# Expert tiles of the first four batches run before the last batches are ranked

## The chip, the cores and the metric

The kernel runs on one core of a Trainium2 chip. Its time is the device time in microseconds, the median of three runs: 293.11 us (292.9 to 294.67). Inputs are those of the reference.

## The reference

A gated block in two steps, on 8 batches of 256 tokens of width 512, all in float32:

```
x = x + tanh(g_xattn) * attention(layernorm(x), ctx, mask)
x = x + tanh(g_ffn)   * experts(layernorm(x))
attention: scores = h @ ctx.T / sqrt(512), -1e30 where masked, softmax, @ ctx
experts:   probs = softmax(y @ w_router.T); the two largest of 8, renormalised
           out = sum over the two of weight * (silu(y @ w_gate[e].T) * (y @ w_up[e].T)) @ w_down[e].T
```

w_gate and w_up are 192 x 512 for each expert, w_down is 512 x 192. Each of the 2048 tokens goes to two experts, so there are 4096 assignments.

## The kernel before

**Two stages.** The first stage runs over 16 tiles of 128 tokens (two a batch), in software-pipelined steps: in step s, tile s is transposed (`t1`), tile s-1 is scored, its row maximum and exponential are taken (`rowmax`, `exp`), tile s-2 has its probabilities transposed and multiplied with the context (`tp`, `pv`), tile s-3 gets the attention result added (`x2`, L655), its second norm (`stats`, `rstd`, `nbias`, `x2ln`) and its transposes (`t2`), and tile s-4 its router logits (`rt`). ScalarE's queue stores each tile of the residual to `out` and each normed tile to a DRAM table `x2s` (L450, L454).

**Ranking.** For each batch b, VectorE finds the two best experts of each token (`top2`, `ranks`), TensorE counts how many earlier assignments an expert has (`cum`), VectorE turns this into a slot number and two one-hot matrices TA and TB (`slots`, L714 and L721), and TensorE sums their products in the PSUM bank PTB (`tab`): a table that gives the token of every slot. `coefs` makes the token's weight for each expert, which SyncE stores in the last 8 columns of `x2s`. On VectorE this work is woven between the operations of the main chain (`weave`, list `side`).

**Second stage.** The slots of an expert are cut in tiles of 128. `tiles` computes from the final counts which expert and which slots each of up to 39 tiles has; this gives the index lists IXG (gather) and IXI (scatter), the experts ER, the live number LN and a bit for each tile whose expert is another than that of the tile before (TN). A tile j is then: a gather of 128 rows of `x2s` into one of 6 buffers XG (GpSimd's queue, L409), four transposes (`tx`, L1063), a split into a high and a low float32r part (`xhi`, `xlo`), twelve products with the gate and up weights (`gu`, L1073, L1074, L1077), SiLU and product (`silu`, `mul`), two transposes (`th`), another split (`hhi`, `hlo`), five products (`down`), scaling on ScalarE (`yev`, into one of 5 buffers YT) and an indirect DMA that adds the tile to `out` (GpSimd's queue, L435). TensorE's order in an iteration is gu(j), tx(j+1), down(j-1), th(j). Since two tiles of different experts can hold the same token, GpSimd waits, where the expert changes, until every earlier add has landed (`fence`, `landed`). After add j GpSimd issues gather j+6.

**Weights.** 40 pieces of 128 x 512 are loaded by SyncE (`loadw`), rounded on ScalarE (`hi`) and the rest of the rounding computed on GpSimd (`lo`, L379). SPLIT says how many fall in each step: two, and four of them only in the second stage (HOLD).

All engines run their programs in order; what sets the order is the code as written, with semaphores.

Of the kernel before, what the change touches and what calls it, by code (L numbers as in the profile page):

```python
# [8 lines left out]
NTK = 16  # L9
# [5 lines left out]
NB = 5  # L15
# [14 lines left out]
def flamingo(nc, x, ctxn, ctxt, mask, gates, wr, wgu, wd1, wd2, cst, cstb, out):  # L30
# [11 lines left out]
    with ctx:  # L42
# [32 lines left out]
        bit = CS[:, 486:525]  # L75
# [39 lines left out]
        Y2 = sb("Y2", [128, 2, D], where=a)  # L115
        Y2T = sb("Y2T", [128, KC, 128], where=a)
        WS = sb("WS", [128, 2, 512], where=a)
        TA = sb("TA", [128, 4, 128], f32r, where=a)
        TB = sb("TB", [128, 4, 128], f32r, where=a)
        mrow = sb("mrow", [B, S], mybir.dt.uint8, where=a)  # L120
        mbf = P[0:B, 0, :]
        mb = sb("mb", [128, S], bf16, where=a)
        gr = sb("gr", [B, 2], where=a)
        gt = sb("gt", [B, 2], where=a)
        va = sb("va", [B, 1], where=a)
        gv = sb("gv", [B, 10], where=a)
        mx = sb("mx", [128, 2, 8], where=a)
        ix = sb("ix", [128, 2, 8], u32, where=a)
        dd = sb("dd", [128, 2, 1], where=a)
        e2 = sb("e2", [128, 2, 1], where=a)  # L130
        den = sb("den", [128, 2, 1], where=a)
        cc = sb("cc", [128, 2, 2], where=a)
        OH = sb("OH", [128, 2, 2, E], where=a)
        pc = sb("pc", [128, 2, 2, E], where=a)
        pr = sb("pr", [128, 2, 2, E], where=a)
        sl = sb("sl", [128, 2, 2], where=a)
        Qi = sb("Qi", [128, 2, 2], i32, where=a)
        rr = sb("rr", [128, 2, 2], where=a)
# [1048 lines left out]
```

## Time and profile before

| what | value |
|---|---|
| median of 3 runs | 293.11 us |
| the profiled execution | 292.34 us |
| its span on the core | 290.5 us |
| TensorE busy | 254.5 us (88%) |
| VectorE busy | 172.3 us (59%) |
| ScalarE busy | 147.4 us (51%) |
| GpSimd busy | 163.8 us (56%) |
| mean granted TensorE clock | 0.944 |

The profile is one execution, timed from the span's start. The first stage takes about 104 us, the second runs from 135 us. Busy shares are means over both; what bounds each stretch is read from the stretch alone.

### The profile page before, as it was taken

The numbers are of one execution on the slowest core, as the hardware profiler recorded it, in microseconds if no ns is written. First come the engines' busy times: TensorE is split into PE (matmuls) and PEld (weight loads), VectorE is DVE, ScalarE is ACT, GpSimd is POOL, SyncE is SP. The second block draws the span as 40 slices with busy tenths as digits, with TensorE's granted clock in tenths as the row PEclk, the third lists the DMA queues.
The fourth block names the chain that finished last, engine by engine and source line by source line (L and its number), as shares of the span: only waits on it lengthen the run. The fifth ranks groups of instructions, "written<-read, shape, count | busy, mean of one in ns | idle before, by whom it ended". The sixth has DMA issues, their size and how long they took to land.

```text
span 290.5 us, 5453 instructions
## 1 busy us (share of the span) xinstructions
PE 254.5 (88%) x1501; PEld 216.1 (74%) x1501; DVE 172.3 (59%) x650; ACT 147.4 (51%) x310; POOL 163.8 (56%) x151
## 2 busy tenths in 40 slices
PE   0999998999999975366999999999999999999940
PEld 1777875687777645356899999899999999999920
DVE  4477779999987899970444444444444554444420
ACT  3469865787765645300455554454444455444430
POOL 1256557556564448316066686874857747748460
PEclk9999999999999978557999999999999999999985
DMA  6996999789988229006157576885985858958582
GB/s 219 381 386 192 325 353 282 295 265 336 301 302 296 82 104 287 4 1 184 38 81 145 103 136 123 143 143 94 171 178 93 168 114 143 154 98 163 109 142 36
DMA packets 25950, 52.08 MB, mean 179 GB/s; under 512 B 5248, under 2 KB 5376, under 8 KB 25920
## 3 DMA queue, kind: packets, MB, share of 16 engines
q0 software_dynamic: 8304, 19.83, 37.0%
q1 hardware_dynamic: 13008, 23.50, 24.7%
q10 hardware_dynamic: 4608, 8.39, 7.6%
q8 instruction: 15, 0.25, 0.3%
q14 instruction: 15, 0.12, 0.2%
HBM read 33.81 MB, written 17.89 MB: 178 GB/s over the span
## 4 chain that ended last, share of the span: by engine, by line
PE 63%; DVE 23%; issue 5%; ACT 3%; DMA 2%; POOL 1%; ACTq 0%; POOLq 0%; DVEq 0%
PE S L1073 9%; PE S L1074 9%; PE S L1077 9%; PE A L1063 5%; PE PO L946 4%; DVE st L609 4%; PE S L935 4%; DVE X L655 3%; DVE TB L721 3%; DVE TA L714 2%; PE PL L1096 2%; DVE dd L675 2%; PE PO L1098 1%; PE PO L1096 1%; PE PL L1100 1%
## 5 line engine op out<-in xcount | busy, mean ns | idle before, releaser
L435 POOL DMA_INDIRECT out<-YT,IXI x36 | 56.8, 1577 | 42.1 <-issue 20.1
L1073 PE MATMUL S<-WGh,XTh 128*128 x144 | 52.3, 363 | 0.9 <-issue 0.8
L1074 PE MATMUL S<-WGl,XTh 128*128 x144 | 49.3, 342 | 0.0
L409 POOL DMA_INDIRECT XG<-x2s,IXG x39 | 38.5, 986 | 18.0 <-issue 9.4
L875 DVE TENSOR_TENSOR H<-SG,S 128x192 f32<-128x192 f32 x36 | 12.7, 354 | 48.5 <-ACT SG L548 40.9
L379 POOL TENSOR_TENSOR WGl<-WGl,WGh 128x512 fp32r<-128x512 f32 x24 | 30.6, 1280 | 14.9 <-ACT WGh L504 14.8
L548 ACT ACTIVATE SG<-S 128x192 f32<-128x192 f32 x36 | 11.9, 330 | 50.3 <-PE S L1077 47.6
L370 POOL TENSOR_TENSOR rs<-mv,CS 128x1 f32<-128x1 f32 x32 | 17.6, 551 | 31.2 <-DVE mv L615 31.2
L946 PE MATMUL PO<-CX,PT 128*128 128x512 f32 x64 | 32.8, 637 | 2.0 <-ACT PT L477 2.0
L868 DVE TENSOR_TENSOR XTl<-A,XTh 128x512 fp32r<-128x512 f32 x37 | 25.6, 691 | 13.0 <-ACT XTh L541 7.9
L1077 PE MATMUL S<-WGh,XTl 128*128 x144 | 31.3, 340 | 0.0
L935 PE MATMUL S<-CT,XLT 128*128 128x256 f32 x128 | 31.0, 386 | 0.0
L1073 PEld LDWEIGHTS S<-WGh,XTh 128*128 128x128 f32 x144 | 27.5, 191 | 1.5 <-issue 1.4
L1074 PEld LDWEIGHTS S<-WGl,XTh 128*128 128x128 f32 x144 | 27.7, 192 | 0.0
L541 ACT ACTIVATE XTh<-A 128x512 fp32r<-128x512 f32 x37 | 22.1, 598 | 8.7 <-PE A L1063 4.3
L1077 PEld LDWEIGHTS S<-WGh,XTl 128*128 128x128 f32 x144 | 26.1, 192 | 0.0
L935 PEld LDWEIGHTS S<-CT,XLT 128*128 128x128 f32 x128 | 23.6, 195 | 2.9
L499 ACT ACTIVATE Y<-X,nb,rs 128x512 f32<-128x512 f32 x16 | 13.0, 812 | 22.7 <-DVE nb L624 22.6
L609 DVE BATCH_NORM_STATS2 st<-X 128x6 f32<-128x512 f32 x32 | 22.0, 688 | 3.9 <-DMA X<-in_x 3.4
L1063 PE MATMUL A<-CS,XG 128*128 128x128 f32 x148 | 22.2, 272 | 1.4 <-DMA XG<-x2s,IXG 1.4
L1063 PEld LDWEIGHTS A<-CS,XG 128*128 128x128 f32 x148 | 18.4, 140 | 2.8 <-issue 1.6
L946 PEld LDWEIGHTS PO<-CX,PT 128*128 128x128 f32 x64 | 11.6, 199 | 10.7 <-issue 8.2
(153 smaller groups left out, 535.8 us busy)
## 6 DMA issues: line engine op xcount, KB each, us to landing
WGl<-in_wgu SPq DMA_DIRECT2D x24, 256.0 KB, 6.2
X<-in_x SPq DMA_DIRECT2D x16, 256.0 KB, 5.3
CT<-in_ctxt SPq DMA_DIRECT2D x8, 512.0 KB, 6.7
CX<-in_ctxn SPq DMA_DIRECT2D x8, 512.0 KB, 5.4
out<-X ACTq DMA_DIRECT2D x16, 256.0 KB, 5.7
x2s<-Y ACTq DMA_DIRECT2D x16, 256.0 KB, 5.2
WD1l<-in_wd SPq DMA_DIRECT2D x8, 256.0 KB, 5.6
WS<-in_wd SPq DMA_DIRECT2D x8, 256.0 KB, 4.6
```

What stands on the lines that cost most here:

```text
L379: pool.tensor_tensor(out=low, in0=raw[p], in1=hi[p].bitcast(fp32), op=ALU.subtract).then_inc(s_wl, 1)
L409: pool.indirect_dma_start(out=XG[:, j % NX, :], out_offset=None, in_=x2s, in_offset=bass.IndirectOffsetOnAxis(ap=IXG[:, j:j + 1], axis=0))\
L435: pool.indirect_dma_start(out=out, out_offset=bass.IndirectOffsetOnAxis(ap=IXI[:, j:j + 1], axis=0), in_=YT[:, j % NB, :], in_offset=None, ...
L541: act.activation(XTh[:, j % 2, :, :], (A0, A1)[j % 2][:, :].rearrange("p (k c) -> p k c", k=KC), ACT.Copy).then_inc(s_xh, 1)
L609: n = mark(dve.bn_stats(st[:, k % 2, :], src))
L868: dve.tensor_tensor(XTl[:, j % 2, :, :], (A0, A1)[j % 2][:, :].rearrange("p (k c) -> p k c", k=KC), XTh[:, j % 2, :, :].bitcast(fp32), ALU ...
L935: m = pe.matmul(SC[k % 2][:, 0:S], XLT[:, k % 2, c, :], CT[:, b % 2, c, :], start=False, stop=(c == KC - 1))
L946: m = pe.matmul(PO[:, :], PT[:, k % 2, c, :], CX[:, b % 2, c, :], start=(c == 0), stop=(c == 1))
L1063: m = pe.transpose((A0, A1)[j % 2][:, 128 * c:128 * c + 128], XG[:, j % NX, 128 * c:128 * c + 128], ident)
L1073: pe.matmul(o, XTh[:, j % 2, c, :], WGh[:, bass.ds(e, 1), c, :], start=(c == 0), stop=False)
L1074: pe.matmul(o, XTh[:, j % 2, c, :], WGl[:, bass.ds(e, 1), c, :], start=False, stop=False)
L1077: m = pe.matmul(o, XTl[:, j % 2, c, :], WGh[:, bass.ds(e, 1), c, :], start=False, stop=(c == KC - 1))
```

## The change

**What it does.** The first four batches (EB = 4) have 2048 assignments over 8 experts. Whatever the routing, at least 16 - 7 = 9 tiles of these are whole (NE = 9). The change makes a first list from the counts and the table after four batches: IXE (rows), ERE (experts), the first nine entries of EJ (weights' columns) and TNE (bits). These nine tiles run first in the second stage; the ranking of batches 4 to 7, the tail of the first stage (`pv(15)`, `rt(13)` to `rt(15)`, `t2(14)`, `t2(15)`) and the second list (`left`, `last_tiles`: up to 30 tiles) run inside tiles 0 to 8. On TensorE they stand at fixed places of the loop over tiles; on VectorE SIDES gives how many operations of the list `side` follow `mul`, `coef` and `hlo` of each tile.

**GpSimd.** Gather 0 stands in step 16, gathers 1 to 5 between the last norms, gather j+8 after add j. Gather 9 is the first that needs the second list (IXG). Before add j GpSimd waits that add j-2 has landed; that add j-1 has landed only where the bit is set: where the expert changes and the last token of tile j is not before the first token of tile j-1. At add 9 it always waits for add 8.

**Weights.** Three pieces a step for 12 steps; none is left for the second stage.

**Small operations.** The factor 1/sqrt(512) is put on ScalarE's eviction of the transposed tile, the maximum is negated by the reduction itself, and the gate of the attention is put on ScalarE's eviction of the probabilities: two VectorE operations of 128 x 1 a tile fewer. For batches 6 and 7 the exponential is made on GpSimd as a power (`odds`).

**Buffers.** Tiles of the second stage use one PSUM bank for `tx` (A0), the bank of `gu` again for `th`, one for `down` (PO); YT has 7 buffers. XG lies on X, so gathers wait for the stores of X's tiles (`stored`). The filling matmuls (`warm`) of the handover are gone.

```diff
-NB = 5
+NB = 7
-SPLIT = [0, 1, 1] + [2] * 15 + [1] * 4
-NUA = NU - 4
-HOLD = [3, 5, 7, 9]
+SPLIT = [0, 1, 2] + [3] * 12 + [1]
+EB = 4
+NE = 4 * EB - 7
+SIDES = [(2, 2, 5), (2, 2, 3), (1, 1, 2), (1, 1, 2), (2, 2, 2), (2, 2, 3), (1, 3, 4), (2, 1, 4)] + [(0, 0, 0)] * 31
...
@@ GpSimd @@
+            for s in range(NTK + 1):
+                for u in units(s - 1)[0:1]:
+                    lo(u)
+                if s == NTK:
+                    pool.wait_ge(s_ixe, 1)
...
+                    stored(9, 10)
+                    gather(0)
...
             for j in range(NT):
                 with lives(pool, live, j):
+                    if j == 1:
+                        odds(7)
                     pool.wait_ge(s_y, j + 1)
-                    if j:
+                    if j >= 2:
+                        landed(j - 2)
+                    if j == NE:
+                        landed(j - 1)
+                    elif j:
                         fence(j)
...
+                    if j == 0:
+                        gather(NX)
+                        gather(NX + 1)
+                    if j + NX + 2 == NE:
+                        pool.wait_ge(s_ixg, 1)
...
+                    if j + NX + 2 < NT:
+                        gather(j + NX + 2)
...
@@ VectorE @@
             def rowmax(k):
                 dve.wait_ge(s_sc, k + 1)
-                n = mark(dve.reduce_max(nmx[:, k:k + 1], SC[k % 2][:, 0:S], AX.X))
-                yield
-                need(n)
-                dve.tensor_scalar(nmx[:, k:k + 1], nmx[:, k:k + 1], -SCALE, None, ALU.mult).then_inc(s_mx, 1)
+                dve.reduce_max(nmx[:, k:k + 1], SC[k % 2][:, 0:S], AX.X, negate=True).then_inc(s_mx, 1)
+                yield
...
+            side += [coefs(5), top2(6), taken()]
+            weave(queue(x2(14), first_xlo(), nbias(mv2, rs2, nb2, 14, s_rs2, s_nb2), x2(15)), 2)
+            side += [slots(5), ranks(6), coefs(6),
+                     braid(slots(6), queue(top2(7), braid(ranks(7), coefs(7)))),
+                     braid(slots(7), left()), last_tiles()]
...
                     mul(j)
+                    steps(SIDES[j][0])
                     if j + 1 < NT:
                         xlo(j + 1)
...
                     coef(j)
+                    steps(SIDES[j][1])
                     hlo(j)
+                    steps(SIDES[j][2])
...
@@ TensorE @@
+            tp(14)
+            first_list()
+            score(15)
+            pv(14)
+            rt(12)
+            t2(13)
+            tp(15)
...
             tx(0)
-            own, live = experts(0), None
+            pv(15)
+            rt(13)
+            own, live = experts(0, ERE, 0), None
+            pe.wait_ge(s_wl, NU)
             for j in range(NT):
                 with lives(pe, live, j):
...
                     gu(j, own[j])
+                    if j == 0:
+                        t2(14)
+                    if j == 1:
+                        t2(15)
+                        rt(14)
                     if j + 1 < NT:
                         tx(j + 1)
+                    if j == 0:
+                        cum(5)
+                    if j == 2:
+                        tab(5)
+                        cum(6)
+                    if j == 4:
+                        cum(7)
+                        count()
+                    if j == 5:
+                        tab(6)
+                    if j == 6:
+                        last_list()
+                        tab(7)
...
                     if j >= 1:
                         down(j - 1, own[j - 1])
+                    if j == 1:
+                        rt(15)
+                    if j == 6:
+                        last_rows()
                     th(j)
+                    if j == 0:
+                        tab(4)
```

**TensorE at the start of the second stage, before.** PTB is the table, sel and selE the one-hot choice of slots for each tile, XG the gathered rows.

```order
L1034 MATMUL PL<-Rn,CB 128x8
L989 MATMUL PTB<-TB,TA 128x128 [waits s_oh] x4
L1039 MATMUL PO<-sel,CS 1x40 [waits s_x2,s_sel]
L1043 MATMUL PC<-sel,Tsb 128x40 [waits s_sel]
L1044 MATMUL PL<-selE,CB 128x320
L910 MATMUL S<-CB 128x128 x32
L1063 MATMUL A<-CS,XG 128x128 [waits s_ixi,s_g0,s_wl,s_er]
L1053 TENSOR_LOAD ER
L1073 ISA [waits s_xh]
L1073 MATMUL S<-WGh,XTh 128x384
```

And in the changed kernel, from the last transposes of probabilities (L1127) on:

```order
L1127 MATMUL S<-CS,P 128x128 [waits s_ex]
L1291 MATMUL A<-CS,XG 128x128 [waits s_ere,s_inc,s_g0,s_eje,s_ixe]
L1150 MATMUL PO<-CX,PT 128x512 [waits s_x2,s_cx1,s_pt]
L1167 MATMUL PL<-WR,Y2T 128x8 [waits s_y2t]
L1281 TENSOR_LOAD ERE
L1301 ISA [waits s_xh,s_wl]
L1301 MATMUL S<-WGh,XTh 128x384
```

The gathered tile 0 is now transposed between two products of the first stage, and the first expert products follow the router logits of tile 13. The sums for all batches stand no longer ahead of them.

**GpSimd's queue in the changed kernel**, from the first add to `out` on (e is the odds of batch 7, IXE the first list, IXG the second):

```order
L486 DMA out<-YT,IXE 2944x512 [waits s_y]
L422 DMA XG<-x2s,IXE 128x520 [waits s_cj,s_tx] x3
L414 TENSOR_TENSOR e<-CS,dd 128x2 [waits s_cb,s_dd]
L438 REGISTER_ALU [waits s_y]
L438 UNCONDITIONAL_BRANCH [waits s_add0]
L486 DMA out<-YT,IXE 2944x512
L422 DMA XG<-x2s,IXG 128x520 [waits s_scb1,s_tx,s_sy1,s_cj,s_sy0,s_ixg]
L438 REGISTER_ALU [waits s_add0,s_y]
L438 UNCONDITIONAL_BRANCH [waits s_add1]
```

Adds 2 and later stand behind gather 9, which waits for IXG.

**VectorE in the changed kernel**, from hlo(5) to xlo(7), with the place at which IXG is made:

```order
L1029 TENSOR_TENSOR HTl<-S,HTh 128x256 [waits s_hh]
L798 TENSOR_SCALAR TB<-CS,rr 128x128
L960 TENSOR_TENSOR Tsb<-PTB,Tsb 128x128 [waits s_tab]
L963 TENSOR_SCALAR IXG<-PC 128x32 [waits s_ixp]
L1023 TENSOR_TENSOR H<-SG,S 128x192 [waits s_th,s_sg]
L1024 TENSOR_TENSOR H<-SG,S 128x64
L965 SCALAR_TENSOR_TENSOR Y2T<-PC,CS 128x32
L1016 TENSOR_TENSOR XTl<-A,XTh 128x512 [waits s_xh]
```

Before, none of these operations but H and XTl was made inside the loop over tiles; IXG now stands ahead of H of tile 6 and behind two TensorE steps of that tile.

## Rows read from the trace of the kernel before

**Rows 1.** Busy time by stretch (busy us of PE, PEld, DVE, ACT, POOL; clock; DMA share; GB/s)

```profile
60.00:96.00 36.00, 35.21 (x214) 26.54 (x211) 31.70 (x138) 25.16 (x57) 20.18 (x23) 1.00 0.86 288
96.00:104.00 8.00, 5.91 (x33) 4.17 (x32) 7.02 (x29) 4.06 (x10) 3.93 (x4) 1.00 0.38 132
115.00:129.00 14.00, 5.56 (x44) 4.56 (x45) 12.49 (x56) 2.21 (x4) 3.55 (x3) 0.50 0.08 23
144.00:278.00 134.00, 133.46 (x783) 122.66 (x781) 62.73 (x207) 66.62 (x141) 91.05 (x71) 1.00 0.71 130
```

**Rows 2.** Timeline of TensorE over the handover (start us, us, then what; [idle before])

```profile
95.73 0.65 PE L989 MATMUL PTB<-TB,TA 128*128 128x128 f32 x4
...
96.21 0.40 PE L923 MATMUL S<-CS,P 128*128 128x128 f32 x2
...
98.29 1.88 PE L946 MATMUL PO<-CX,PT 128*128 128x512 f32 x4
...
100.55 1.03 PE L965 MATMUL PL<-WR,Y2T 128*128 128x8 f32 x8 [0.37 <-DVE ix L668]
101.43 0.63 PE L954 MATMUL A<-CS,Y 128*128 128x128 f32 x4
...
104.29 3.60 PE L946 MATMUL PO<-CX,PT 128*128 128x512 f32 x4 [2.01 <-ACT PT L477]
...
127.89 0.65 PE L1043 MATMUL PC<-sel,Tsb 128*128 128x40 f32 x2 [0.38 <-DVE Tsb L848]
...
134.73 0.57 PE L1073 MATMUL S<-WGh,XTh 128*128 x1 [0.77 <-issue]
...
139.85 0.44 PE L1073 MATMUL S<-WGh,XTh 128*128 x1
```

**Rows 3.** VectorE's timeline in step 16: tile 13's sum, tile 15's maximum

```profile
95.41 0.74 DVE L655 SCALAR_TENSOR_TENSOR X<-PO,rinv,X 128x512 f32<-128x512 f32 x1
...
99.44 0.40 DVE L630 TENSOR_REDUCE nmx<-S 128x1 f32<-128x256 f32 x1
```

**Rows 4.** Granted clock of a stretch of the handover (columns as in Rows 1)

```profile
104.40:107.60 3.20, 3.20 (x4) 1.41 (x5) 2.81 (x11) 1.03 (x2) 1.78 (x2) 0.50 0.18 68
```

**Rows 5.** Timeline of VectorE and GpSimd, two operations side by side

```profile
98.13 1.27 POOL L379 TENSOR_TENSOR WGl<-WGl,WGh 128x512 fp32r<-128x512 f32 x1
...
98.32 1.11 DVE L740 TENSOR_TENSOR comb<-pc 128x16 f32<-128x16 f32 x1
```

**Rows 6.** VectorE by line, one of the two groups that the change removes

```profile
L647 DVE TENSOR_TENSOR rinv<-rinv,GB 128x1 f32<-128x1 f32 x16 | 2.5, 157 | 0.2
```

**Rows 7.** A stretch of the first stage with full DMA (columns as in Rows 1)

```profile
76.00:82.00 6.00, 6.00 (x33) 4.32 (x31) 5.97 (x22) 3.84 (x11) 3.47 (x4) 1.00 1.04 390
```

**Rows 8.** Timeline of TensorE in the second stage: a tile's first product, its transposes, the next tile's

```profile
199.01 0.42 PE L1073 MATMUL S<-WGh,XTh 128*128 x1
...
201.19 0.60 PE L1063 MATMUL A<-CS,XG 128*128 128x128 f32 x4
...
202.94 0.42 PE L1073 MATMUL S<-WGh,XTh 128*128 x1
```

**Rows 9.** GpSimd's first gather and TensorE's first transposes of it

```profile
129.66 1.18 POOL L409 DMA_INDIRECT XG<-x2s,IXG  x1 [6.47 <-DVE IXG L850]
...
133.33 0.63 PE L1063 MATMUL A<-CS,XG 128*128 128x128 f32 x4 [1.41 <-DMA XG<-x2s,IXG]
```

**Rows 10.** GpSimd's timeline in the second stage: adds, the third behind a fence, and the last

```profile
209.79 1.58 POOL L435 DMA_INDIRECT out<-YT,IXI  x1 [0.30 <-issue]
...
212.95 1.58 POOL L435 DMA_INDIRECT out<-YT,IXI  x1 [0.30 <-issue]
...
219.03 1.57 POOL L435 DMA_INDIRECT out<-YT,IXI  x1 [3.21 <-issue]
...
282.30 1.55 POOL L435 DMA_INDIRECT out<-YT,IXI  x1 [1.65 <-ACT YT L562]
```

**Rows 11.** The costliest groups: the adds

```profile
L435 POOL DMA_INDIRECT out<-YT,IXI x36 | 56.8, 1577 | 42.1 <-issue 20.1
```

More of the change, by code:

```diff
@@ L408, in gather @@
                     pool.wait_ge(s_cj, j - NX + 1)
-                pool.indirect_dma_start(out=XG[:, j % NX, :], out_offset=None, in_=x2s,
-                                        in_offset=bass.IndirectOffsetOnAxis(ap=IXG[:, j:j + 1], axis=0))\
+                rows, at = (x2s[0:EB * S, :], IXE[:, j:j + 1]) if j < NE else (x2s, IXG[:, j - NE:j - NE + 1])
+                pool.indirect_dma_start(out=XG[:, xg(j), :], out_offset=None, in_=rows,
+                                        in_offset=bass.IndirectOffsetOnAxis(ap=at, axis=0))\
@@ L425, in _ @@
+            stored(11)
+            gather(1)
+            rstd(mv2, 14, rs2, s_st2, s_rs2)
+            stored(12)
+            gather(2)
+            rstd(mv2, 15, rs2, s_st2, s_rs2)
+            odds(6)
+            stored(13)
+            gather(3)
+            pool.wait_ge(s_tne, 1)
+            early = pool.value_load(TNE[0:1, 0:1], min_val=0, max_val=(1 << 13) - 1)
+            stored(14, 15)
+            for j in range(4, NX):
                 gather(j)
-            pool.wait_ge(s_tn, 1)
@@ L434, in _ @@
                         fence(j)
-                    pool.indirect_dma_start(out=out, out_offset=bass.IndirectOffsetOnAxis(ap=IXI[:, j:j + 1], axis=0),
-                                            in_=YT[:, j % NB, :], in_offset=None, compute_op=ALU.add)\
+                    to = IXE[:, j:j + 1] if j < NE else IXI[:, j - NE:j - NE + 1]
+                    pool.indirect_dma_start(out=out, out_offset=bass.IndirectOffsetOnAxis(ap=to, axis=0),
+                                            in_=yt(j), in_offset=None, compute_op=ALU.add)\
@@ L456, in _, with store_x2 @@
+            def store_x2(k):
+                act.wait_ge(s_x2, k + 1)
+                act.dma_start(rows(out, k), X[:, k % NXT, :]).then_inc(s_so[k % NXT], 16)
             act.wait_ge(s_m, 32)
@@ new lines, in steps, with first_xlo @@
+            def steps(n):
+                for _ in range(n):
+                    while side and next(side[0], side) is side:
+                        side.pop(0)
+            def first_xlo():
+                xlo(0)
+                yield
+            side += [coefs(5), top2(6), taken()]
[3 more added lines that the diff above has]
+                     braid(slots(7), left()), last_tiles()]
@@ L1005, in _ @@
                     pe.wait_ge(s_mb, 1)
-                if 0 <= s - 1 < NTK:
+                if s >= 1:
                     score(s - 1)
+                if s == 2 * EB + 5:
+                    tab(EB - 2)
+                    cum(EB - 1)
                 if s == 1:
@@ L1046, in _ @@
-            warm(32)
-            pe.wait_ge(s_er, 1)
-            pe.wait_ge(s_wl, NUA)
-            pe.wait_ge(s_ixi, 1)
-            def experts(j):
+                if s >= 3:
+                    t2(s - 3)
+                if s >= 7 and s % 2 == 1 and s != 2 * EB + 5:
+                    cum((s - 7) // 2)
+                if s >= 9 and s % 2 == 1 and s < 2 * EB + 5:
+                    tab((s - 9) // 2)
+                if s == 2 * EB + 6:
+                    tab(EB - 1)
+            tp(14)
```

680 lines of the change are left out of this document (413 added, 267 removed).

## The prediction
> **What bounds the kernel now.** I read busy time by stretch first. In 60 to 96 us TensorE is busy 35.21 of 36 us and VectorE 31.70; in 144 to 278 us TensorE is busy 133.46 of 134 us and VectorE 62.73 [rows 1]. Both stages are bound by TensorE. Between them it is not: it is busy 5.56 us in 115 to 129 us, at half clock, while VectorE is busy 12.49 of 14 us with the ranking [rows 1]. The timeline says the same: the product with context of tile 14 starts at 98.29 us, the first expert product at 134.73 us [rows 2]. Of these 36 us the first stage needs only some 12. A steady tile takes 202.94 - 199.01 = 3.93 us [rows 8].
>
> The second thing to see is GpSimd's queue. It has 36 adds [rows 11]. Back to back, two adds start 212.95 - 209.79 = 3.16 us apart; at a fence they start 219.03 - 212.95 = 6.08 us apart, the time in which the earlier add lands [rows 10]. The reference's routing gives 36 tiles with 7 changes of expert; 7 fences and 28 plain steps make 131 of the 137.5 us between the first add (5 us behind the second tile's first product, 139.85 us [rows 2]) and the last at 282.30 us [rows 10]. GpSimd is thus nearly a second bound of the second stage.
>
> **Part 1: when the first expert product starts.** I walk through step 16 in the new order. The transposes of tile 14's probabilities start at 96.2 us [rows 2]. The four products of the first list have 9 to 12 columns in place of 40; by the 0.65 us of one with 40 columns at half clock [rows 2] I give all four 1.1 us. VectorE then makes IXE and only after it adds tile 13: at 97.8 instead of 95.41 us [rows 3]. From there to tile 15's maximum it took 99.44 - 95.41 = 4.0 us [rows 3]; now the slots of batch 4 and four reads of the first list are woven in, some 13 operations more, among them TA and four TB. I take 6.0 us for it, and the maximum at 103.8 us; exponential and transposes end at 105.5 us, tx(0) at 106.1 us. The gather is in time: it is issued at about 98 us, and took 133.33 - 129.66 = 3.7 us [rows 9]. Then come pv(15) with 1.9 us, rt(13) with 1.0 us [rows 2] and the load of the experts: gu(0) at 109.5 us.
>
> In this walk TensorE is idle for about 2.5 us before tp(15). Before, after 2.01 us of idle time, the product of tile 15 took 3.60 instead of 1.88 us [rows 2], at a granted clock of 0.50, the 1.2 GHz level [rows 4]. I add this 1.7 us once: 111.2 us.
>
> **Part 2: the first stage with three weight pieces a step.** GpSimd's 1.27 us operation held VectorE: a sum of 128 x 16, started beside it at 98.32 us, took 1.11 us and ended with it [rows 5]; such a sum else takes about 0.16 us, as its like [rows 6]. A blocked operation costs 0.94 us, and about every second piece meets one: +0.47 us of VectorE a step. The two operations that go give back 2 x 0.157 = 0.31 us [rows 6]. Net +0.16 us for each of 12 steps, 2.0 us, which I count whole since VectorE's full stretches (5.97 of 6 us [rows 7]) have no room. Bounds: TensorE keeps the pace alone, 0; every piece blocks, (0.94 - 0.31) x 12 = 7.6 us. DMA is alike: 288 GB/s now [rows 1], 262 KB more each 6 us makes 332, and 390 GB/s is what a full stretch moved [rows 7]; 85% should pass, though loads of X wait for stores of X. So gu(0) is at 113.2 us, 21.5 us earlier than 134.73.
>
> **Part 3: what moves into the tiles.** TensorE gets two t2 (0.63 us each), two rt (1.03 each), four tab (0.65 each) [rows 2], three cum with the count (0.9 together) and the products of the second list (1.0), both estimated as the first list was. That is 7.8 us by durations that hold some overlap with the next operation; I take 7.3 (bounds 6 and 9). Their cover was idle time; here TensorE has none, so all of it counts. In tile 6 VectorE makes Tsb and IXG ahead of H(6), and IXG waits for last_rows, which waits for Tsb and stands behind down(5): TensorE then waits for IXG and H(6), about 1.0 us (0 to 3). Side operations elsewhere lie in VectorE's idle half [rows 1] and cost nothing; without that cover each 0.16 us would. Against this, the first tile took 139.85 - 134.73 = 5.1 us at half clock [rows 2] and should now take its 3.9: -1.2 us. The small operations of ScalarE (a scale on an eviction that is there anyway) and the changed banks I cost at nothing: gu(j) and down(j) wait for what is over 1 us old in the steady tile.
>
> **Part 4: GpSimd behind gather 9.** This is what is late next. Gather 9 waits for IXG, and adds 2 and later stand behind it. By part 3 tile 7 starts 7 x 3.93 + 7.3 + 1.0 = 35.8 us after gu(0), and IXG is ready some 0.9 us before, at 34.9 us. Gather 9 takes 2.2 us with its wait, so add 2 starts at 37.1, four tiles late. Gather j+8 is issued 1.9 us after add j and usable 3.7 us after its issue, and must be there for tx(j+8), 201.19 - 199.01 = 2.2 us into tile j+7 [rows 8, 9]. For add 2: 37.1 + 5.6 = 42.7 against 35.8 + 2 x 3.93 + 2.2 = 45.9, so 3.2 us are in hand. A plain step wins 3.93 - 3.16 = 0.77 us, a fence loses 6.15 - 3.93 = 2.2 us (6.15 is the mean of the fences; [rows 10] has 6.08).
>
> Which fences remain follows from the inputs. Routed by the reference, the first half has 288, 223, 147, 239, 382, 318, 300 and 151 assignments by expert, so the nine tiles are 0, 0, 1, 2, 3, 4, 4, 5, 5: their tokens overlap at each change, at tiles 2, 3, 4, 5 and 7. At the later changes the new expert's tile starts and ends before the old one's last tile, so six of seven fences go; one before the padded tile (25) stays, and the fixed wait at tile 9. From add 2 to add 9: 3.2 + 2 x 0.77 - 5 x 2.2 = -6.3 us. TensorE waits that long in all, in pieces of up to 2.3 us; as in part 1 a piece of that length may halve the clock, 1.0 us. From there on the backlog shrinks. The wait for the landing of add j-2 is met at 2 x 3.16 = 6.3 us. The chain of adds itself ends at 37.1 + 6 x 6.15 + 27 x 3.16 = 159 us after gu(0), and 290.5 - 282.3 = 8.2 us follow: 280.7 us with part 2, just under what TensorE gives.
>
> **The sum.** -21.5 + 7.3 + 1.0 - 1.2 + 6.3 + 1.0 = -7.1 us on the span of 290.5: 283.4. The profiled execution was 292.34 us, so 285.2; the median of the runs is 0.8 us above that, so 293.11 - 7.1 = 286.0. I forecast **286 us**. A measurement here tells about 1% from no change, so below 290.2 is faster, above 296.0 slower.
>
> **The rivals.**
>
> *Gathers are in time.* If IXG comes 6 us earlier, or fences are shorter, the fences eat only what is in hand; if also the clock holds over the handover, 6.3 + 1.0 + 1.7 go: 277 us. For it: the 0.80 us that TensorE lacks in 60 to 96 us [rows 1] shows that VectorE's blocks are mostly hidden. Against: IXG hangs on the place of last_rows in tile 6. Chance 0.22.
>
> *The first stage slows.* Every piece blocks VectorE, or DMA at 332 of 390 GB/s [rows 1, 7] makes loads of X late: the upper bound of part 2, 5.6 us more, 291.6 us, no change. For it: VectorE is at 5.97 of 6 us beside a DMA share of 1.04 [rows 7]. Chance 0.14.
>
> *Adds land later.* The end on the other side. The adds of the second list now run with a backlog, and each waits for the landing of the one before the last. Up to 6.3 us for a landing this costs nothing; from there it sets the pace. At 7.0 us, plain steps take 3.5 us and fences 7.0: 37.1 + 6 x 7.0 + 27 x 3.5 = 174, plus 8.2 and 113.2, a span of 295.4, 298 us. For it: 6.08 us [rows 10] is only 0.2 us below that point. Against: it was measured behind adds that were back to back too. Chance 0.10, which holds also fences that I count as gone, at 3 us each.
>
> *The early start does not come.* The first gather waits for stores, the first list, the comb columns of batch 3; if one of them is 7 us late, a third of part 1 is gone and the moved TensorE work stays: 293 us. For it: in the first stage SyncE's queue is long. Against: the DMA share in 96 to 104 us is 0.38 [rows 1]. Chance 0.03.
>
> *VectorE holds up GpSimd's issues.* TA, TB and their like run on VectorE beside gathers 0 to 8 now. Seen so far is only the other direction [rows 5]. If gather 0 and gather 9 wait as long as VectorE did there, 0.94 us each, 288 us. The Trainium skill says it outright (SBUF - State Buffer, "SBUF: two separate sides"): a DMA issued from GpSimd cannot get its descriptors written while VectorE runs an operation that takes both ports. By that rule these gathers wait; no run here shows it yet. Chance 0.03.
>
> The forecast has 0.48. Its own spread is 281 to 290.5. **Range** 276 to 295 us: it leaves out the last of adds landing later and the lower end of gathers in time. **Chances:** faster 0.74 (forecast, gathers in time, held issues, and a few in a hundred of the first-stage case), same 0.16, slower 0.10.
>
> **What would show it.** Part 1: first expert product (L1301) at 111 to 116 us, with a clock of 0.5 for some 3 us before it. Part 2: the transposes of tile 14 at 98 us; a first stage of over 6.3 us a step would be the second rival. Part 3: tiles 0 to 6 in 33 to 38 us, tile 1 the longest. Part 4: in the timeline of GpSimd a wait of over 10 us before gather 9, then adds at 6.1 us at tiles 3, 4, 5, 7, 9; on TensorE waits for XG in tiles 11 to 17. If TensorE never waits for XG there, the first rival holds. If adds come at over 3.3 us in the plain steps, the third. I am wrong altogether if the second stage's steady tile is not 3.9 us.

## The result, and the profile after

The changed kernel takes **296.79 us** (median of 4 runs, 296.14 to 297.64), the kernel before 293.0 on the same chip: ratio 1.0127, 95% interval 1.0095 to 1.0159. It is slower by over 1%; I had forecast 286, with a range to 295. The profiled execution has a span of 294.5 us against 290.5.

Busy time by stretch, kernel after (columns as in [rows 1]):

```profile
20.00:60.00 40.00, 37.00 (x197) 27.78 (x195) 29.39 (x102) 30.61 (x65) 27.96 (x29) 0.96 0.92 315
60.00:96.00 36.00, 28.60 (x165) 21.21 (x165) 28.42 (x107) 19.96 (x42) 20.03 (x20) 0.91 0.80 260
115.00:129.00 14.00, 12.16 (x75) 9.05 (x73) 10.26 (x53) 6.55 (x13) 6.59 (x7) 1.00 0.40 128
144.00:200.00 56.00, 51.92 (x317) 46.32 (x316) 29.39 (x122) 23.44 (x50) 23.33 (x19) 1.00 0.47 88
```

In 60 to 96 us TensorE was busy 35.21 of 36 us before [rows 1] and is busy 28.60 now, at a mean clock of 0.91; VectorE is less busy too. Neither engine bounds the first stage any more: they wait for each other. DMA moves less than before, 260 GB/s. At 115 to 129 us, once the hole between the stages, TensorE is now busy 12.16 of 14 us at full clock.

Timeline of TensorE and VectorE over the handover, after: probabilities of tile 14, tile 13's sum, first expert product, that of the second tile:

```profile
115.38 0.42 PE L1127 MATMUL S<-CS,P 128*128 128x128 f32 x2
...
116.44 0.74 DVE L732 SCALAR_TENSOR_TENSOR X<-PO,rinv,X 128x512 f32<-128x512 f32 x1
...
126.77 0.42 PE L1301 MATMUL S<-WGh,XTh 128*128 x1
...
132.44 0.39 PE L1301 MATMUL S<-WGh,XTh 128*128 x1
```

The forecast had 98.2 and 113.2 us in place of 115.38 and 126.77. The first stage is 17.2 us later than forecast, the walk from there to the first expert product 3.6 us shorter (11.4 for 15.0), and the rest 2.5 us shorter (from that product to the span's end 167.7 for 170.2). The sum, 11.1 us, is the whole error on the span (294.5 against 283.4).

Starts of the sums `x2` on VectorE (us), and where the 21.0 us at tile 13 arise; the last two rows are two of the experiments below:

| kernel | tile 9 | tile 11 | tile 13 | tiles 9 to 11 |
|---|---|---|---|---|
| before | 71.06 | 83.38 | 95.41 | 12.3 |
| after | 79.13 | 102.17 | 116.44 | 23.0 |
| two pieces a step (e2) | 70.73 | 91.19 | 105.61 | 20.5 |
| narrow remainders (e4) | 72.14 | 92.45 | 105.47 | 20.3 |

So 8.1 us are lost up to tile 9, spread over the steps, 10.7 at once between tiles 9 and 11 (steps 12 and 13), and 2.2 behind.

**The even loss.** What the engines waited for in 20 to 60 us (engine, line, releaser: us in total, times, longest), kernel before and then after:

```profile
DVE nb L624 <- POOL rs L370: 1.6, 2, 0.8
ACT Y L499 <- DVE nb L624: 10.1, 7, 2.8
PEld A L954 <- ACT Y L499: 3.7, 5, 1.6
```

```profile
DVE nb L706 <- POOL rs L396: 7.2, 5, 2.5
ACT Y L562 <- DVE nb L706: 8.8, 5, 3.0
PEld A L1158 <- ACT Y L562: 4.4, 3, 2.6
```

VectorE waits 5.6 us more for GpSimd's power `rs`, which stands in GpSimd's queue behind the pieces. ScalarE's norm, which waits behind VectorE, does not wait longer than before (8.8 for 10.1 us), and the weights of TensorE's transposes wait 0.7 us longer.

Waiting is not all. From tile 0's sum to tile 9's VectorE and TensorE have the same work in the changed kernel with two pieces a step (e2 below) and with three (columns as in [rows 1]):

```profile
18.79:70.73 51.94, 50.84 (x292) 38.09 (x291) 42.91 (x165) 38.40 (x82) 30.49 (x35) 1.00 0.89 307
```

```profile
19.18:79.13 59.95, 53.24 (x292) 39.50 (x291) 48.25 (x166) 42.57 (x90) 42.15 (x44) 0.97 0.92 312
```

Of the 8.0 us more, 5.3 are VectorE's own operations, which take longer beside the pieces, and 2.7 are idle time. Its wait for the power grows by more than that, but its waits for ScalarE's exponential and for TensorE's product shrink. In this stretch the changed kernel is also once at half clock: TensorE was idle for 1.74 us before 49.25 us, and the granted clock was 0.50 in 51 to 53 us.

**The jumps.** Timeline of steps 12 and 13, after (TensorE and VectorE in order of time):

```profile
86.06 1.85 PE L1167 MATMUL PL<-WR,Y2T 128*128 128x8 f32 x8 [3.69 <-DVE ix L745]
87.76 3.67 PE L1150 MATMUL PO<-CX,PT 128*128 128x512 f32 x4
...
91.54 0.75 DVE L732 SCALAR_TENSOR_TENSOR X<-PO,rinv,X 128x512 f32<-128x512 f32 x1 [4.28 <-PE PO L1150]
...
94.99 0.19 DVE L775 TENSOR_TENSOR pr<-OH,PC 128x32 f32<-128x32 f32 x1 [1.97 <-PE PC L1190]
...
100.55 0.21 DVE L706 TENSOR_SCALAR nb<-mv,rs 128x1 f32<-128x1 f32 x1
...
101.66 1.12 PE L1158 MATMUL A<-CS,Y 128*128 128x128 f32 x4 [3.99 <-ACT Y L562]
```

The router product waits for the ranking of batch 3 (`ix`), which the new order put behind the slots of batch 2. After the idle time TensorE ran at half clock (0.50 in 86 to 91 us, the 1.2 GHz level), the product with the context took 3.67 in place of 1.9 us, and VectorE waited for it in turn. One step later VectorE stands in front of the count (`PC`) while the statistics that the norm needs queue behind it. Their power is ready at 96.97 us, but `nb`, which the norm needs too, starts only at 100.55: eight woven operations start in between, one of them held for 1.25 us. TensorE's next transposes come 3.99 us late, again at half clock (1.12 for 0.60).

**The second stage** did nearly what was forecast. GpSimd's timeline, after:

```profile
161.34 1.01 POOL L422 DMA_INDIRECT XG<-x2s,IXG  x1 [11.63 <-ACT WS L600]
162.65 1.60 POOL L486 DMA_INDIRECT out<-YT,IXE  x1 [0.30 <-DVE cj L1037]
...
168.33 1.58 POOL L486 DMA_INDIRECT out<-YT,IXE  x1 [2.79 <-DMA out<-YT,IXE]
```

Gather 9 waited 11.63 us. The profile puts this down to ScalarE's WS, which ended last before it; IXG, which the gather needs, was made on VectorE at 160.88 us. The gather came 34.6 us after the first expert product (forecast 34.9), add 2 35.9 us (37.1), with fences behind it at the forecast tiles (3, 4, 5, 7 and 9).

### The profile page after: what moved, and what is told of

Its sections match the earlier page's. It is cut to its first block, busy times and chain, and to the rows that moved or that the text cites. A ratio compares the mean times of both kernels' runs of the same rounds, so it can differ in the third digit from the quotient of the medians.

```text
span 294.5 us, 5373 instructions
## 1 busy us (share of the span) xinstructions
PE 253.4 (86%) x1464; PEld 213.1 (72%) x1464; DVE 170.0 (58%) x645; ACT 148.5 (50%) x308; POOL 166.6 (57%) x153
## 4 chain that ended last, share of the span: by engine, by line
PE 52%; DVE 18%; DMA 9%; POOL 8%; issue 5%; ACT 3%; SPq 2%; ACTq 0%; POOLq 0%; DVEq 0%
PE S L1301 7%; PE S L1305 7%; PE S L1302 7%; PE A L1291 5%; PE PO L1150 4%; DVE st L691 4%; DMA XG<-x2s,IXG 3%; PE PO L1322 3%; DVE TB L798 3%; DMA WGl<-in_wgu 3%; DVE X L732 3%; POOL WGl L405 3%; PE PO L1327 2%; PE PO L1326 2%; PE PO L1324 2%
## 5 line engine op out<-in xcount | busy, mean ns | idle before, releaser
L1301 PE MATMUL S<-WGh,XTh 128*128 x144 | 51.5, 357 | 0.0
L1302 PE MATMUL S<-WGl,XTh 128*128 x144 | 48.3, 336 | 0.0
L396 POOL TENSOR_TENSOR rs<-mv,CS 128x1 f32<-128x1 f32 x32 | 18.5, 578 | 43.6 <-DVE mv L697 43.6
L422 POOL DMA_INDIRECT XG<-x2s,IXG x30 | 29.7, 988 | 20.5 <-ACT WS L600 11.6
L486 POOL DMA_INDIRECT out<-YT,IXI x19 | 30.1, 1587 | 16.5 <-issue 8.4
L1139 PE MATMUL S<-CT,XLT 128*128 128x256 f32 x128 | 32.9, 403 | 0.0
L1139 PEld LDWEIGHTS S<-CT,XLT 128*128 128x128 f32 x128 | 25.3, 209 | 3.5
L600 ACT ACTIVATE YT<-PO,cj 128x512 f32<-128x512 f32 x26 | 17.9, 688 | 18.8 <-PE PO L1327 15.5
L1029 DVE TENSOR_TENSOR HTl<-S,HTh 128x256 fp32r<-128x256 f32 x36 | 15.3, 424 | 20.1 <-ACT HTh L592 15.8
```

The costliest lines, as they stand in the source:

```text
L422: pool.indirect_dma_start(out=XG[:, xg(j), :], out_offset=None, in_=rows, in_offset=bass.IndirectOffsetOnAxis(ap=at, axis=0))\
L486: pool.indirect_dma_start(out=out, out_offset=bass.IndirectOffsetOnAxis(ap=to, axis=0), in_=yt(j), in_offset=None, compute_op=ALU.add)\
L1139: m = pe.matmul(SC[k % 2][:, 0:S], XLT[:, k % 2, c, :], CT[:, b % 2, c, :], start=False, stop=(c == KC - 1))
L1301: pe.matmul(o, XTh[:, j % 2, c, :], WGh[:, bass.ds(e, 1), c, :], start=(c == 0), stop=False)
L1302: pe.matmul(o, XTh[:, j % 2, c, :], WGl[:, bass.ds(e, 1), c, :], start=False, stop=False)
```

## The experiments

e1 to e9, e11 and c4 were run once; e10 and c1 to c3 four to ten times, and their runs spread over 3 to 5 us. The kernel before took 293.87 us beside e1 to e4, 292.08 beside e5 to e8, 292.78 beside e9 to e11 and c1, and 292.99 beside c2 to c4. A difference of 2 or 3 us between two single runs is therefore read from the starts of the sums: in the three traces with the same first stage, the changed kernel's, e7's and e9's, these agree within 0.7 us at tile 9 (78.43 to 79.13) and within 0.9 us at tile 13 (115.82 to 116.74).

**e1: the weight schedule alone.**

```diff
-SPLIT = [0, 1, 1] + [2] * 15 + [1] * 4      # kernel before
+SPLIT = [0, 1, 2] + [3] * 12 + [1]          # and no HOLD
```

> The kernel before with the changed kernel's weight schedule alone: three pieces a step for 12 steps, none in the second stage. Measure: the start of the sum of tile 13 (95.41 us in the kernel before, 116.44 in the changed one). If three pieces a step are what slows the first stage, whether by GpSimd's rounding operations, by the loads or by SyncE's queue, the sum of tile 9 comes at 77 to 79 us (71.06 before, 79.13 changed) and that of tile 13 at 103 to 116 us; the time is then 300 to 312 us. If it is the order of the ranking in steps 12 and 13, this kernel does not have it: tile 9 at 71 to 73 us, tile 13 at 95 to 98 us, and the time within 3 us of 293.

Measured: 298.74 us; tile 9 at 84.18, tile 13 at 112.37. Three pieces a step slow the first stage without any other part of the change, by 13.1 us up to tile 9, more than I expected (8.1 in the changed kernel, which has two small operations fewer). Of the 5.0 us between them 2.8 can be put down to one of these two, the product with the gate (`rinv`): beside a piece it was held itself, for 0.91, 1.07 and 1.25 us in place of 0.16. The delay shrinks to 8.3 us at the first expert product; no pieces fall in the last steps here.

**e2: the changed kernel with two pieces a step.**

```diff
-SPLIT = [0, 1, 2] + [3] * 12 + [1]
+SPLIT = [0, 1, 1] + [2] * 12 + [14]
```

> The changed kernel with two pieces a step through step 14 and the other 14 pieces at the end of the first stage; only the pace up to tile 13 counts, the end pays for the late pieces. If three pieces a step are the whole cause, the sum of tile 9 comes at 71 to 72 us and that of tile 13 at 95 to 98 us. If the order of steps 12 and 13 (slots of batch 2 ahead of the ranking of batch 3, counting of batch 3 ahead of the router product) has its own part, tile 9 comes at 71 to 72 us but tile 13 at 101 to 106 us. If the small operations that went to ScalarE slow the stage, tile 9 is already over 74 us.

Measured: tile 9 at 70.73, tile 13 at 105.61 (299.73 us, with the late pieces). The even loss is the pieces', all of it. Of the jumps 8.1 us stay (20.5 for 12.3). There are two causes.

**e3: another order in steps 12 and 13.**

```diff
-if s == 2 * EB + 5: tab(EB - 2); cum(EB - 1)     # TensorE, ahead of rt
+# both at the end of the step; on VectorE slots(2) behind top2(3),
+# slots(3) and whole() one step later, and two woven operations for one
+# (weave) only from step 14 on, not from step 12
```

> The changed kernel with the ranking of batch 3 ahead of the slots of batch 2 on VectorE, and TensorE's count of batch 3 back at the end of step 13; three pieces a step stay. If the order has its own part, the jumps of 12.4 and 10.6 us between the sums of tiles 9, 10 and 11 shrink to 7 to 8 us, tile 13 comes at 105 to 109 us in place of 116.44, and the time is 286 to 290 us, unless the first list then comes too late for the first gather. If the jumps come from the weights alone (SyncE stood 11.4 us on one load at 74 us), they stay and the time is 294 to 298 us.

Measured: 292.49 us; tiles 9 to 11 take 15.3 us, but 11 to 13 then 17.4, tile 13 at 110.98, between the two expectations. The order has its own part; part of what it gave came back in the steps that the slots were postponed to.

**e4: narrow remainders.**

```diff
-pool.tensor_tensor(out=low, in0=raw[p], in1=hi[p]...)
+n = 512 if half else 32
+pool.tensor_tensor(out=low[:, 0:n], in0=raw[p, 0:n], in1=hi[p, 0:n]...)
```

> The changed kernel with GpSimd's rounding remainder computed on 32 of 512 columns for 32 of the 40 pieces (the other remainders are left out); loads and ScalarE's part are as they were. If GpSimd's 1.27 us operations, which hold VectorE and stand ahead of the norms' power, are what slows the stage, the sums come 6.0 to 6.3 us apart, tile 9 at 71 to 73 us and tile 13 at 95 to 103 us, and the time is 275 to 284 us. If it is the volume of loads or SyncE's queue, tile 9 stays at 77 to 79 us and the time above 292 us.

Measured: 285.15 us, with most of the remainders left out; tile 9 at 72.14, while the loads are whole (332 GB/s in 20 to 60 us). So 7.0 of the 8.1 us are GpSimd's computing time. Tiles 9 to 11 still take 20.3 us, which I had not written down for it.

**e5: pieces issued a step later by SyncE.**

```diff
-for u in units(s + 2): loadw(u)
+for u in units(s + 1): loadw(u)
```

> The changed kernel with SyncE issuing each step's weight pieces one step later, so that no load of X or of the context stands behind a piece that waits for GpSimd; everything else as in the changed kernel. If SyncE's queue, which stood 11.4 us on one load at 74 us, makes the first stage late, the sums come sooner: tile 13 at 108 to 113 us in place of 116.44, the time at 289 to 293 us. If the queue is only long beside other causes (GpSimd's operations and the order of the ranking), tile 13 stays within 1.5 us of 116.4 and the time within 2 us of 296.8; pieces that land later could even cost 1 to 3 us.

Measured: 296.92 us, tile 13 at 117.29. SyncE's queue, which I had suspected since it stood 11.8 us on two loads at 73.7 us, is not what bounds the changed kernel. The edit has a cost of its own, though: the sum of tile 0 comes at 20.80 for 19.18 us, and from there to tile 13 the run takes 0.8 us less than the changed kernel.

**e6: VectorE's order alone.**

```diff
+side.append(top2(3)) ahead of side.append(slots(2))          # step 12
+weave(queue(*main), True, hold=3)   # step 13: nothing woven in before the statistics
```

> The changed kernel with two edits of VectorE's order and none of TensorE's: in step 12 the ranking of batch 3 stands ahead of the slots of batch 2, and in step 13 the operations woven in begin only after the second norm's statistics. With two pieces a step, tiles 9 to 11 still took 20.5 us, as with narrow remainders (20.3), against 12.3 in the kernel before; in the last experiment on the order they took 15.3, but the two after them 17.4. If TensorE's wait for the ranking (2.96 us) and VectorE's for the count (2.33 us), each with half clock behind it, are the whole of these 8 us, tiles 9 to 11 take 14 to 16 us here and tiles 11 to 13 14 to 15 us: tile 13 at 108 to 110 us, time 288 to 290 us. If the doubled share of woven operations is what costs, tiles 9 to 11 take over 18 us and the time is above 293 us.

Measured: 290.98 us; tiles 9 to 11 18.1 us, more than the first expectation, tile 13 at 110.47. The wait for the ranking went, step 12 takes 8.0 us for 12.4; step 13 still took 10.1. VectorE's timeline shows a new wait there:

```profile
92.09 0.69 DVE L691 BATCH_NORM_STATS2 st<-X 128x6 f32<-128x512 f32 x1 [3.13 <-DMA X<-in_x]
```

and SyncE's, the load in front of it:

```profile
73.00 12.38 SPq L337 DMA_DIRECT2D WS<-in_wd  x2
```

The second of these two pieces may start only when GpSimd has finished an earlier one; all loads behind it wait. **e11** adds later loads from step 8 on:

```diff
-for u in units(s + 2): loadw(u)
+for u in units(s + 2) if s < 8 else units(s + 1) if s > 8 else (): loadw(u)
```

> The changed kernel with the two edits of VectorE's order in steps 12 and 13, and SyncE's weight pieces from step 8 on issued one step later. With the order alone (289.2 us span), VectorE waited 3.13 us for a load of X in step 13, behind SyncE's wait for GpSimd. If SyncE's queue is the next cause in line and was hidden by the order, that wait goes: step 13 takes 7 to 8 us in place of 10.1, tile 13 comes at 107 to 109 us in place of 110.47, the time is 287 to 289 us. If the queue never mattered, as in the run with later loads alone (tile 13 at 117.29 against 116.44), the time stays at 290 to 292 us.

Measured: 288.63 us, step 13 8.8 us, tile 13 at 107.99. Tiles 9 to 13 take 29.4 us for 31.4 in e6. The queue was a cause after all, hidden behind the order; e5, which moved the loads of every step, showed 0.8 us of it at most. Tiles 9 to 11 still take 16.9 us for the 12.3 of the kernel before, so the two waits were not all: c4 below, without GpSimd's computing, still takes 14.5.

**e8: the norms' power ahead of the third piece.**

```diff
-for u in units(s - 1)[1:]: lo(u)
-rstd(mv1, s + 2, ...)
+for u in units(s - 1)[1:2]: lo(u)
+rstd(mv1, s + 2, ...)
+for u in units(s - 1)[2:]: lo(u)
```

> The changed kernel with one edit of GpSimd's order: the power for the first norm of tile s+2 stands ahead of the third weight piece of a step in place of behind it. VectorE waited 7.2 us for this power in 20 to 60 us (1.6 in the kernel before). If most of the cost of three pieces is that the norms queue behind them, the sum of tile 9 comes at 73 to 75 us (79.13 changed, 70.73 with two pieces) and the time at 290 to 293 us. If it is that each piece holds VectorE's own operations, wherever it stands, tile 9 stays at 77 to 80 us.

Measured: 293.11 us; tile 9 at 77.32, in the range of the second expectation. VectorE's wait for the power falls from 7.2 to 3.3 us in 20 to 60 us, but its operations take longer. From tile 0's sum to tile 9's:

```profile
18.82:77.32 58.50, 53.59 (x299) 39.46 (x297) 50.22 (x165) 43.01 (x91) 42.45 (x45) 0.97 0.93 323
```

That is 2.0 us more of VectorE's time than in the changed kernel (48.25) and 3.4 less idle, 1.5 in all. One step of this run, GpSimd's timeline and then VectorE's:

```profile
58.42 1.26 POOL L405 TENSOR_TENSOR WD<-WS,WD 64x512 fp32r<-64x512 f32 x1
...
60.48 1.27 POOL L405 TENSOR_TENSOR WGl<-WGl,WGh 128x512 fp32r<-128x512 f32 x1
61.92 1.27 POOL L405 TENSOR_TENSOR WGl<-WGl,WGh 128x512 fp32r<-128x512 f32 x1 [0.17 <-ACT WGh L569]
```

```profile
58.49 1.22 DVE L769 TENSOR_TENSOR Rt<-Rn,MS 128x8 bf16<-128x8 bf16 x1
...
60.53 1.24 DVE L812 TENSOR_TENSOR cc<-cc,e 128x2 f32<-128x2 f32 x1
...
62.03 1.20 DVE L819 TENSOR_TENSOR comb<-pc 128x16 f32<-128x16 f32 x1
```

Each of the three pieces holds one operation of 0.16 us until it ends. So both mechanisms are there: one queues, one holds. Taking the queue away returns 1.5 of the 8 us, since a piece that no longer delays the power holds an operation in its place.

**e7 and e9: what stands ahead of gather 9.**

```diff
-after add j: gather j + 8            # gather 9 after add 1
+e7: gathers 9, 10, 11 after add 4, gathers 12, 13 after add 5
+e9: gathers 9, 10, 11 after add 3
```

> The changed kernel with the adds of tiles 2 to 4 issued ahead of gather 9, which alone waits for the second list; gathers 9 to 11 follow add 4 and gathers 12 and 13 add 5. If the backlog behind gather 9 is what lets TensorE wait 6.0 us for rows in tiles 11 to 17, these waits go: tiles 9 to 18 come 3.93 us apart and the second stage, first product to last, takes 145 us in place of 150.8; time 290 to 292 us. If the pace of GpSimd's adds and fences as such limits, not where they start, over half of the 6 us stays and the time is 294 us or more.

> The changed kernel with adds 2 and 3 issued ahead of gather 9, and gathers 9 to 11 between adds 3 and 4; from add 4 on the old order. In the run with adds 2 to 4 ahead, gather 9 came at 40.7 us after the first product, 5 us late, because the fenced adds before it come 5.9 us apart. If the start of gather 9 is what matters and the fences are only the pace behind it, gather 9 comes here at 35 to 36 us after the first product, later gathers keep ahead of TensorE, and its waits for rows in tiles 8 to 18 fall from 6 us to 0 to 2 us: the second stage, first to last product, takes 145 to 147 us, the time 291 to 293 us. If the adds' pace limits in any order, the waits stay at 4 to 6 us and the time at 295 us or more.

Measured: e7 297.76 us, e9 290.22. GpSimd's timeline of e7, then of e9:

```profile
155.42 1.57 POOL L486 DMA_INDIRECT out<-YT,IXE  x1 [4.24 <-DMA out<-YT,IXE]
161.23 1.54 POOL L486 DMA_INDIRECT out<-YT,IXE  x1 [4.25 <-DMA out<-YT,IXE]
167.08 1.55 POOL L486 DMA_INDIRECT out<-YT,IXE  x1 [4.31 <-DMA out<-YT,IXE]
168.94 1.03 POOL L422 DMA_INDIRECT XG<-x2s,IXG  x1 [0.30 <-issue]
```

```profile
158.88 1.54 POOL L486 DMA_INDIRECT out<-YT,IXE  x1 [4.06 <-DMA out<-YT,IXE]
160.73 1.02 POOL L422 DMA_INDIRECT XG<-x2s,IXG  x1 [0.30 <-DVE IXG L964]
```

In e7 a third fenced add pushes gather 9 to 40.7 us after the first product, and TensorE waits 3.7 us once for its rows, so that first to last product still take 150.7 us. In e9 it comes at 34.6 us with two adds already out; TensorE never waits for rows, and first to last product take 144.9 us for 150.8.

**e10: the small operations alone, on the kernel before.**

```diff
-dve.tensor_scalar(nmx, nmx, -SCALE, ...)    # negate=True in the reduction
-dve.tensor_tensor(rinv, rinv, GB, ...)      # scale=GB on ScalarE's eviction
```

> The kernel before with the small operations alone: the negation by the reduction, the factor on ScalarE's eviction of the transposed tile, the gate on its eviction of the probabilities. If two operations of 0.16 us fewer on VectorE, which was busy 5.97 of 6 us in a full stretch, shorten each step, tile 13 comes up to 3 us sooner and the ratio is 0.990 to 0.995. If TensorE keeps the pace alone, tile 13 stays at 95.4 us within 0.5 us and the ratio is 0.998 to 1.001. If the wait for GB or the scaled copies cost ScalarE time on the path, it is over 1.002.

Measured: ratio 0.9963, interval 0.9933 to 0.9994; tile 13 at 94.18, 1.2 us sooner. Between the two expectations: a small gain.

**c1 to c4: all edits together, and what is left.** c1 = e11 + e8 + e9. c2 spreads the pieces as [0, 1, 3, 4, 4] + [3] * 6 + [2] * 5; c3 cuts each subtraction in two of 256 columns; c4 is c1 with e4's edit, which leaves out most of the remainders.

> The changed kernel with all edits that bore on a cause: VectorE's order in steps 12 and 13, later loads of pieces from step 8 on, the norm's power ahead of the third piece, and gathers 9 to 11 between adds 3 and 4. If the parts add up (5.8 us for the order, 2 to 3 for the queue, 3.7 for the power, 4 to 5 for the gathers), the time is 278 to 282 us, 4 to 5% below the kernel before. If each edit only uncovers the same limit, VectorE's operations held by GpSimd, it is 284 to 290 us.

> The combined kernel (281.7 us) with the same 40 pieces spread otherwise: 3, 4 and 4 in steps 2 to 4, three in steps 5 to 10, two from step 11 on. If a piece costs only where VectorE has ranking to do, as steps of 5.5 to 5.9 us up to tile 4 and of 7.4 to 7.8 us behind it say, the early steps stay at 5.5 to 6 us, the five late ones lose 0.5 to 1 us each, and the time is 277 to 280 us. If SyncE's queue or the loads cannot take four pieces a step, the first tiles come late by 2 to 5 us and the time is 282 to 286 us.

> The combined kernel with each of GpSimd's 128 x 512 subtractions cut in two of 128 x 256. If VectorE is let in between two GpSimd operations, a held operation waits at most for a half, so held ones take up to 0.65 us in place of 1.0 to 1.25 and the full steps fall from 7.7 to 7.0 us: 277 to 280 us. If it gets no turn between them, or two short ones hold twice as many operations, the time stays within 1.5 us of 281.7.

> The combined kernel with the remainder computed on 32 of 512 columns for 32 of the 40 pieces (the other remainders are left out). If GpSimd's time beside VectorE is all that is left of the first stage's loss, the steps to tiles 5 to 9, 7.4 to 7.8 us, fall to 6.0 to 6.3, tile 13 comes at 95 to 99 us in place of 106.11, and the time is 271 to 275 us. If loads or SyncE's queue hold a part, tile 13 stays above 101 us.

| run | us | ratio to before | tile 9 | tile 13 | first product |
|---|---|---|---|---|---|
| c1 | 281.68 | 0.9627 (0.9566 to 0.9688) | 76.68 | 106.11 | 117.41 |
| c2 | 282.50 | 0.9632 (0.9561 to 0.9703) | 80.72 | 108.10 | 120.27 |
| c3 | **278.11** | 0.9477 (0.9420 to 0.9533) | 74.95 | 104.78 | 116.23 |
| c4 | 272.37 | one run | 70.13 | 97.21 | 108.87 |

The parts nearly add up: 5.8 + 2.4 + 3.7 + 6.6 = 18.5 us off 296.8 would be 278.3, 3.4 below c1. c2 gives nothing over c1, as its second expectation had it: its late steps are shorter (12 and 13 take 7.1 and 7.8 us for 8.1 and 8.6), but tile 4 comes 8.8 us after tile 3, where VectorE waited 1.24 us for a load of X and then TensorE 1.60 us for the ranking. c3 is the best kernel. In it GpSimd's and VectorE's timelines read:

```profile
60.77 0.72 POOL L406 TENSOR_TENSOR WGl<-WGl,WGh 128x256 fp32r<-128x256 f32 x1
61.53 0.73 POOL L405 TENSOR_TENSOR WGl<-WGl,WGh 128x256 fp32r<-128x256 f32 x1
```

```profile
60.87 0.67 DVE L818 TENSOR_TENSOR pc<-OH,cc 128x32 f32<-128x32 f32 x1
61.58 0.71 DVE L822 TENSOR_TENSOR comb<-pc 128x16 f32<-128x16 f32 x1
```

A held operation waits for a half piece, 0.67 to 0.71 in place of 1.2 us. c4 in 40 to 80 us (columns as in [rows 1]):

```profile
40.00:80.00 40.00, 39.65 (x248) 30.64 (x247) 33.86 (x146) 32.16 (x69) 15.93 (x33) 1.00 0.96 337
```

TensorE is busy all the time beside 337 GB/s of transfers. What c1 still loses there, 6.6 us up to tile 9 and 8.9 up to tile 13, is GpSimd's computing.

## Why the prediction was wrong

**Part 2 failed**: "Net +0.16 us for each of 12 steps, 2.0 us", bounds 0 to 7.6; measured +19.2 us at the transposes of tile 14 (115.38 against 96.21 [rows 2]).
- The held operations were priced too low. I had +0.47 us a step; from e2 to the changed kernel VectorE's same operations took 5.3 us more in nine steps, 0.59 a step. Up to tile 9's sum, 6 of its short operations took over 0.58 us before (6.8 us together; their like take 0.13 to 0.34) and 12 after (13.8 us).
- The credit for the two small operations, 0.31 us a step, hardly came: with two pieces a step TensorE was busy nearly all the time, and from tile 0's sum to tile 9's e2 takes 51.94 us for 52.44 before, 0.06 a step. e10 has 1.2 us up to tile 13.
- Not in the sum at all was GpSimd's queue, and with it any idle time of VectorE: 2.7 us, 0.30 a step. The power `rs` of both norms stands between the pieces, and VectorE stands for it in order. I had counted the change's GpSimd work by what it blocks, not by what queues behind it, though Part 4 did so for the second stage. 0.59 - 0.06 + 0.30 = 0.83 us a step is what the change cost up to tile 9, where I had 0.16. The upper bound, 7.6, was for twelve steps with a held operation in each; e1 lost 13.1 us up to tile 9.
- Nor did I price the order of steps 12 and 13. Part 1 walked through step 16 and took steps up to 15 as they were; there the change had moved the ranking of batch 3 behind the slots of batch 2, and the count ahead of the router product; it also weaves in two operations for one from step 12 on. e2 and e4 put 8 us on all this together, e3, e6 and e11 show where. Both moves stood in the changed kernel; the waits that they make were left out.
- DMA, "85% should pass", was right: c4 carries 337 GB/s at full pace. Single loads of X did come late, 3.13 us in e6 and 1.24 in c2.

**Part 1** was right in kind, too dear by 3.6 us. TensorE's longest idle time there was 1.46 us and the clock stayed at 1.00; the half clock that I had added (1.7 us) did not come. That was luck: with the same 1.46 us before the same transposes the clock went to 0.50 in e8, c1, c3 and c4. In c4 the product of tile 15 then reads (1.98 us in the changed kernel):

```profile
104.89 3.34 PE L1154 MATMUL PO<-CX,PT 128*128 128x512 f32 x4 [0.24 <-ACT PT L544]
```

The gather was in time.

**Part 3** held: tiles 0 to 6 took 35.1 us (35.8), the longest tile 6 with 6.11, where I had put a wait for IXG and H(6) of about 1 us, and not quite tile 1, which I had named, with 6.03.

**Part 4** held: TensorE lost 5.9 us in tiles 11, 12, 14 and 16 to the late gathers (forecast 6.3), without the extra 1.0 for the clock; e9 gave back 5.9 us. Adds came 3.17 to 3.19 us apart in plain steps and some 5.9 at fences.

**The rivals.** "The first stage slows" named the right place and, in the held operations, one of its causes, but neither the queue for the power nor steps 12 and 13, and its price (5.6 us, 291.6) was far too low. "Gathers in time" and "adds land later" did not happen. "VectorE holds up GpSimd's issues": gathers 0 and 1 took 1.17 and 1.23 us to issue beside the ranking, later ones 0.95 to 1.01, the first gather before 1.18 [rows 9]; no wait of 0.94 us shows. The rule of the Trainium skill (SBUF - State Buffer, "SBUF: two separate sides") that such an issue starves beside certain VectorE operations is thus worth at most 0.3 us a gather here (1.23 for 0.95). Its other rule in that section, that the port pair which the two engines share is locked for a whole instruction, the trace agrees with: held operations end with the piece, and with half pieces after 0.67 us.

What stays open: how the 10.7 us of steps 12 and 13 divide between the two moves, the denser weaving and SyncE's queue, since e3, e6 and e11 each left a part of them, and none changed the weaving alone. How much of the 2.7 us of idle time up to tile 9 is the power and how much the half clock at 50 to 54 us is not separated either. And why a load of X came late in c2 was not taken apart.

## What to carry to other kernels

When work is added to an engine off the critical path, price two things besides its busy share: which operations of another engine it holds, and what queues behind it on its own engine and who waits for that in order. Here the first was 5.3 of 8 us, the idle time, which holds the second, 2.7, and removing part of the second let the first grow. Count such operations over the same work, not over the same time: in 20 to 80 us they are 8 before and 12 after, up to the same tile 6 and 12. Where two woven orders meet (VectorE's ranking, TensorE's waits for it), walk through every step that the change touches, since one late small operation cost its wait, a half-clock product and the next engine's wait. If heavy pieces must stand beside short operations, cut them, as c3 did (3.6 us off c1); and if undoing one cause alone shows nothing, try it again with the others gone.

## What the runs showed of the hardware

VectorE's operation was held not only with two operands in SBUF. In the changed kernel one whose only tensor is in SBUF was held as well, beside pieces at 96.93 to 99.41 us:

```profile
98.20 1.25 DVE L843 TENSOR_SCALAR sel<-CS,jq 128x9 f32<-128x9 f32 x1
```

The norms' statistics, the maxima and the sum that reads PSUM were not (0.69, 0.41 and 0.75 us throughout). Nor was a product with one operand in PSUM, at 68.26 us beside a piece of 68.22 to 69.49, while one of the same shape with both in SBUF was:

```profile
39.19 1.27 DVE L757 TENSOR_TENSOR OH<-CS,ix 128x32 f32<-128x32 f32 x1
...
68.26 0.17 DVE L775 TENSOR_TENSOR pr<-OH,PC 128x32 f32<-128x32 f32 x1
```

And the length of TensorE's idle time did not tell whether its clock would fall. In the changed kernel it fell to half after waits of 1.74, 3.69 and 3.99 us, but not after 1.46 or 2.57 us. After the same 1.46 us it fell in c4 (0.50 in 105 to 107 us), after the same 2.57 us in e3 (0.50 in 79 to 82 us), and in e8 after 1.30 us (the next product took 3.28 in place of 1.9 us). So my 1.7 us for it in Part 1 could only be a chance, not a term.
